# A decoder layer on one core: filter matrices kept in SBUF, v left unflipped, and half of the triangular inversion moved into the turns of the next phase

## What is computed

```python
q_in = silu(causal_dwconv(hidden_states @ Wq, wq_conv))        # the same for k_in and v_in
beta = jax.nn.sigmoid(hidden_states @ Wb)
# delta rule in chunks of 32 tokens, per batch and head:
inv = -(kb @ jnp.swapaxes(k, -1, -2)) * strict_lower
for i in range(1, chunk):
    inv = inv.at[..., i, :].add(jnp.einsum('...j,...jk->...k', inv[..., i, :], inv))
inv = inv + jnp.eye(chunk, dtype=q.dtype)
u = inv @ v
w = inv @ kb
...
local_long = causal_dwconv(v_in, fir_long.reshape(-1, fir_long.shape[-1])).reshape(B, L, H, dv)    # 64 taps
local_short = causal_dwconv(v_in, fir_short.reshape(-1, fir_short.shape[-1])).reshape(B, L, H, dv) # 5 taps
stats = jnp.concatenate([head_stats(t) for t in (local_short, local_long, delta_out, v_direct)], -1)
```

## Time and profile before

| | |
|---|---|
| time, median of 3 runs | 1316.88 us (1316.56 to 1321.13) |
| the profiled execution's own time | 1323.56 us |
| its span in the trace | 1321.8 us |
| granted PE clock, mean over the span | 0.895 of full speed |
| phase A, until the first instruction of B | 240.7 us |
| phase B | 240.7 to 319.5 us |
| phase CX, turns 0 and 1 | 319.5 to 362.4 us |
| busy share of the span | PE 85%, DVE 72%, ACT 68%, POOL 49% |

### The profile page before, as it was taken

The page is one execution under the profiler, slowest core; times in us unless marked ns, Lnnn a source line. Parts: engine busy times, 40 slices in busy tenths (PEclk is TensorE's granted clock), DMA queues, the critical chain, the costliest instruction groups (busy, mean ns, idle before and its releaser), DMA issues. The chain is left out here.

```text
span 1321.8 us, 28637 instructions
## 1 busy us (share of the span) xinstructions
PE 1119.9 (85%) x9251; PEld 820.2 (62%) x9251; DVE 958.0 (72%) x2132; ACT 898.0 (68%) x1743; POOL 653.0 (49%) x2200
## 2 busy tenths in 40 slices
PE   5998988783678799999999999999999888885756
PEld 4776766683566566766776776676677655443225
DVE  5999998698355657777877877777787566633985
ACT  5999998221344558787878878877887665453867
POOL 4777775563225544465465466547546543111007
PEclk9999998555557869999999999999999988897989
DMA  2443433893412434343433434343442342203106
GB/s 80 159 176 144 177 136 144 185 234 107 137 57 85 110 80 127 95 124 109 133 110 106 146 105 138 106 129 105 111 144 82 96 127 57 65 33 140 44 1 223
DMA packets 141779, 154.17 MB, mean 117 GB/s; under 512 B 48040, under 2 KB 106560, under 8 KB 141632
## 3 DMA queue, kind: packets, MB, share of 16 engines
q1 hardware_dynamic: 141632, 152.35, 38.4%
HBM read 93.32 MB, written 58.72 MB: 115 GB/s over the span
## 5 line engine op out<-in xcount | busy, mean ns | idle before, releaser
L2120 DVE TENSOR_REDUCE x_maxima<-x_psA 128x2 f32<-128x512 f32 x248 | 170.3, 687 | 96.2 <-PE x_psA L1448 93.7
L1704 ACT ACTIVATE x_PT<-x_psB 128x512 f32<-128x512 f32 x240 | 143.0, 596 | 56.5 <-PE x_psB L1472 52.1
L1711 ACT ACTIVATE x_psA<-x_mask_q 128x512 f32<-128x512 bf16 x239 | 142.4, 596 | 51.8 <-DVE x_maxima L2120 48.7
L297 DVE SCALAR_TENSOR_TENSOR a_conv<-a_ps_proj,taps,a_conv 128x253 f32<-128x253 f32 (+2 forms) x288 | 115.0, 471 | 8.4 <-ACT a_conv L364 8.4
L1448 PE MATMUL x_psA<-x_Ks,x_Qs 96*128 96x256 bf16 x496 | 99.5, 283 | 15.2 <-ACT x_psA L1711 14.7
L1469 PE MATMUL x_psB<-x_mask_k,x_ident_bf 128*128 128x512 bf16 x240 | 94.3, 393 | 13.0 <-ACT x_PT L1704 10.8
L533 PE MATMUL a_ps_proj<-a_hT,wqkv 128*128 128x256 f32 x384 | 93.2, 392 | 7.1 <-DVE a_conv L297 4.2
L1472 PE MATMUL x_psB<-x_Qs,x_Ks 98*128 98x256 bf16 x480 | 94.1, 277 | 0.0
L533 PEld LDWEIGHTS a_ps_proj<-a_hT,wqkv 128*128 128x128 f32 x384 | 71.5, 194 | 19.4 <-issue 6.6
L1864 POOL TENSOR_SCALAR x_parts_q<-x_rest 128x512 bf16<-128x512 f32 x16 | 23.9, 1494 | 116.3 <-DVE x_rest L2096 116.3
L1486 PE MATMUL x_psO<-x_PT,x_V 128*32 128x256 f32 x1024 | 72.0, 401 | 1.0 <-ACT x_PT L1704 1.0
(11 more groups left out here) (390 smaller groups left out, 3352.8 us busy)
## 6 DMA issues: line engine op xcount, KB each, us to landing
scratch_keypack<-a_keypack SPq DMA_DIRECT2D x16, 768.0 KB, 3.3
c_keypack<-scratch_keypack SPq DMA_DIRECT2D x16, 768.0 KB, 4.7
x_Ks<-scratch_k_parts SPq DMA_DIRECT2D x192, 64.0 KB, 2.2
b_matrix<-in_long_padded SPq DMA_DIRECT2D x16, 512.0 KB, 7.4
scratch_k_parts<-x_parts_k SPq DMA_DIRECT2D x32, 192.0 KB, 2.4
scratch_q_parts<-x_parts_q SPq DMA_DIRECT2D x32, 192.0 KB, 2.3
x_Qs<-scratch_q_parts SPq DMA_DIRECT2D x32, 192.0 KB, 3.0
a_x_in<-in_x SPq DMA_DIRECT2D x16, 256.0 KB, 2.7
```

Source lines behind the costliest of these rows:

```text
L297: nc.vector.scalar_tensor_tensor(acc, ps_proj[PROJ_BANK[p]][:, c, 0:L - j], taps[:, p, c, TAPS - 1 - j:TAPS - j], acc, ALU.mult, ALU.add). ...
L1704: nc.scalar.activation(PT[:, k % (2 * GROUP)], bank_B(b, k)[0], ACT.Exp, scale=XD ** -0.5).then_inc(pexp_ready, 1)
L1711: nc.scalar.activation(psA[:].rearrange("p t q -> p (t q)"), mask_q[:, k % 2].rearrange("p s k -> p (s k)"), ACT.Copy).then_inc(mask_writt ...
L2120: nc.vector.tensor_reduce(maxima[:, t, 2 * pair:2 * pair + 2], bank_A(b, k)[0], AX.X, ALU.max).then_inc(maxed, 1)
```

## The change

Four things are changed together.

1. In phase A v is no longer flipped: the two constants, `flipA`, `flipB`, `fA` and `fB` are gone. `vtok` copies straight into `v_windows`, and two SBUF-to-SBUF DMAs per turn (`win`) put the shifted half in place.
2. Phase A also brings the filter's matrices into SBUF, where they stay (`keep["matrix"]`, 256 channels x 64): in turns 1 to 4 one DMA each (`copy`) writes 16 copies of the padded taps to DRAM, and after that two DMAs per turn (`taps0`, `taps1`, 32 in all) read 256 KB each into 16 partitions in pieces of 256 bytes.
3. Phase B's filter has no loads any more. It is 256 matmuls (512 records) whose moving operand is 64 columns wide instead of 32 and whose stationary operand keeps its shape; the two channel halves alternate between the halves of the array's columns. ACT still copies 16 groups. `long` is stored in 8 DMAs of 512 KB in two stages, and B doesn't wait for them; SP waits before it loads `long` for batch 0 in CX, which now stands behind the 20 constant loads.
4. Phase B inverts groups 0 and 1 only, both on DVE as two interleaved single chains. The mask and the diagonal are 63 small memsets per group on POOL, which has no chain any more. Groups 2 and 3 are inverted in CX by DVE as a pair, in the pieces that `LATE_STEPS` lists, over turns 0 to 4.

```diff
-A_ORDER = [(0, "ld_x"), (4, "silu_v"), (1, "rstd"), (5, "kpk"), ...
+A_ORDER = [(0, "ld_x"), (1, "copy"), (4, "silu_v"), (1, "rstd"), (5, "kpk"), ...
...
+                elif op == "copy" and b < COPY_PARTS:
+                    first = b * D // COPY_PARTS
+                    sp.dma_start(dram["taps_copies"][first:first + D // COPY_PARTS],
+                                 bass.AP(dram["long_padded"].tensor, first * FIR_COLS,
+                                         [[FIR_COLS, D // COPY_PARTS], [0, COPIES], [1, FIR_COLS]])).then_inc(taps_copied[b * FC // COPY_PARTS], 16)
+                elif op in ("taps0", "taps1"):
+                    row, half = b % STEP, b // STEP
+                    first = half * P + int(op[-1]) * HB
+                    sp.wait_ge(taps_copied[half], 16 * COPY_PARTS // FC)
+                    taps_of = bass.AP(dram["taps_copies"].tensor, first * COPIES * FIR_COLS + P - 1 - row,
+                                      [[FIR_COLS - STEP, COPIES], [COPIES * FIR_COLS, HB], [1, HB]])
+                    sp.dma_start(keep["matrix"][row:P:STEP, first:first + HB], taps_of).then_inc(taps_placed, 16)
+                elif op == "win":
+                    sp.wait_ge(v_tok_ready, b + 1)
+                    sp.dma_start(keep["v_windows"][HB:P, 0, :, b], keep["v_windows"][0:HB, 1, :, b]).then_inc(window_set, 16)
+                    sp.dma_start(keep["v_windows"][0:HB, 0, 1, b], keep["v_windows"][HB:P, 1, 0, b]).then_inc(window_set, 16)
...
-                    nc.scalar.activation(v_tok[:], ps_tok[2][:], ACT.Copy).then_inc(v_tok_ready, 1)
-                elif op == "fA":
-                    act.wait_ge(v_flipped, b + 1)
-                    nc.scalar.activation(keep["v_windows"][:, 1, :, b], ps_tok[2][:], ACT.Copy).then_inc(flip_kept, 1)
...
+                    nc.scalar.activation(keep["v_windows"][:, 1, :, b], ps_tok[2][:], ACT.Copy).then_inc(v_tok_ready, 1)
...
-CG = 16
-GROUPS = D // CG
-DEPTH = 4
+EARLY_GROUPS = 2
+CHAIN_STEPS = 2 * (CH - 2)
+def substitution(M, product, j):
+    n, rows = M.shape[1], CH - 1 - j
+    return (product[:, :, 0:rows * j].rearrange("p q (i j) -> p q i j", j=j), M[:, :, j + 1:CH, 0:j],
+            M[:, :, j + 1:CH, j:j + 1].broadcast_to([P, n, rows, j]), M[:, :, j:j + 1, 0:j].broadcast_to([P, n, rows, j]))
+CG = 8
+GROUPS = P // CG
+DEPTH = 8
...
+            for stage in range(2):
+                sp.wait_ge(kept, (stage + 1) * (GROUPS // 2))
+                for half in range(FC):
+                    for part in range(2):
+                        at = slice(half * P + stage * HB, half * P + stage * HB + HB)
+                        sp.dma_start(dram["long_tok"][part * HB:part * HB + HB, :, :, at].rearrange("p t b c -> p (t b) c"),
+                                     keep["long"][half * HB:half * HB + HB, part, :, stage * HB:stage * HB + HB]).then_inc(long_stored, 16)
...
-                pe.wait_ge(loaded[n], 16 * (group // DEPTH + 1))
...
-                    for part in range(2):
-                        last = nc.tensor.matmul(psum[n][part * HB:part * HB + HB, c].rearrange("p t b -> p (t b)"),
-                                                matrix[n][:, c], keep["v_windows"][:, part, :, :, group * CG + c].rearrange("p t b -> p (t b)"),
+                for i in range(CG):
+                    for half in range(FC):
+                        c = half * P + group * CG + i
+                        last = nc.tensor.matmul(psum[n][half * HB:half * HB + HB, i], keep["matrix"][:, c],
+                                                keep["v_windows"][:, :, :, :, c].rearrange("p a t b -> p (a t b)"),
...
+            for q in range(EARLY_GROUPS):
+                pool.wait_ge(M_turned, q + 1)
+                for i in range(CH):
+                    nc.gpsimd.memset(M[q][:, i, i:i + 1], 1.0)
+                for i in range(CH - 1):
+                    last = nc.gpsimd.memset(M[q][:, i, i + 1:CH], 0.0)
+                last.then_inc(upper_cleared, 1)
...
+        LATE_STEPS = {(0, "b"): (1, 4), (1, "r"): (4, 9), (1, "d"): (9, 14), (1, "a"): (14, 15), (1, "s"): (15, 16), (2, "p"): (16, 17),
+                      (2, "d"): (17, 19), (2, "a"): (19, 21), (3, "k"): (21, 22), (3, "x"): (22, 23), (3, "q"): (23, 25),
+                      (3, "d"): (25, 26), (3, "a"): (26, 28), (3, "s"): (28, CH - 1)}
...
-            sp.dma_start(long[0][:], dram["long_tok"][:, :, 0]).then_inc(vs_loaded[0], 16)
...
+            sp.wait_ge(early["long_stored"], 128)
+            sp.dma_start(long[0][:], dram["long_tok"][:, :, 0]).then_inc(vs_loaded[0], 16)
...
+                    elif (b, op[3]) in LATE_STEPS:
+                        dve.wait_ge(inverse_step, LATE_GROUPS)
+                        for j in range(*LATE_STEPS[b, op[3]]):
+                            out, below, left, row = substitution(M, product, j)
+                            if j > 1:
+                                dve.wait_ge(inverse_step, LATE_GROUPS + 2 * j - 2)
+                            nc.vector.tensor_tensor(out, left, row, ALU.mult).then_inc(inverse_step, 1)
+                            dve.wait_ge(inverse_step, LATE_GROUPS + 2 * j - 1)
+                            nc.vector.tensor_tensor(below, below, out, ALU.add).then_inc(inverse_step, 1)
```

More of the change, by code:

```diff
@@ new lines, in _ @@
+            dve.wait_ge(M_turned, EARLY_GROUPS)
+            for j in range(1, CH - 1):
+                steps = [substitution(M[q][:].unsqueeze(1) if q == 0 else M[q].unsqueeze(1), products[q].unsqueeze(1), j) for q in range(EARLY_GROUPS)]
+                for q, (out, below, left, row) in enumerate(steps):
+                    if j > 1:
+                        dve.wait_ge(chain[q], 2 * j - 2)
+                    nc.vector.tensor_tensor(out, left, row, ALU.mult).then_inc(chain[q], 1)
+                for q, (out, below, left, row) in enumerate(steps):
+                    dve.wait_ge(chain[q], 2 * j - 1)
+                    nc.vector.tensor_tensor(below, below, out, ALU.add).then_inc(chain[q], 1)
@@ L805 @@
 MASKED = -1e30
-XW_LOADS = 16 * 7
+XW_LOADS = 16 * (7 + 13)
 STACKS = 2
```

258 lines of the change are left out of this document (107 added, 151 removed), and 18 rows, old and new, of the table C_ORDER.

## The result

The changed kernel takes 1309.06 us (median of 13 runs, 1303.55 to 1313.83), the kernel before 1317.64 (13 runs, 1315.10 to 1322.56). The ratio is 0.9929, 95% interval 0.9916 to 0.9942: 9 us faster, where 31 were forecast. The time lies outside the range of 1273 to 1306. The two profiled executions differ by more than the medians, 13.1 us in their spans, because that of the kernel before was 6.7 us longer than its median.

A forecast was written before the change was run, and what follows sets the result against it. The prediction took DVE's inversion to bound phase B, with PE's filter under it. Phase A -1.5, B -41 and CX +11.5 summed to -31 us: 1316.9 - 31 = 1286 us, range 1273 to 1306.

The forecast's parts named there:

- What bounds the kernel: Phase B: bound by DVE's inversion, busy 77.72 of 78.80 us, with PE's filter lying under it.
- inside the turns this is worth nothing: Phase A: removing PE records and ACT copies gains nothing within turns, only about 1.5 us after the last.
- cost 0: Phase A: the added SP issues and 512 KB of DMA per turn were priced at no time.
- The slow rival: Phase A, 3%: extra DMAs delay the load of x; landing 11.1 us after issue gives 1324 us.
- DVE's 37.8 us: Phase B: DVE's transposes, two interleaved chains, constants and a wait sum to 37.8 us against 78.7, a change of -41.
- by that row the moving columns cost nothing extra: Phase B filter: a CX row of the same shape gives 54 ns per record, so 512 records take 27.5 us.
- The filter rival: Phase B, 8%: moving columns set PE's pace, 107 ns per record, 55 us; B about 60 us, the whole 1308.
- The rival of late stores: Phase B into CX, 12%: at half the old rate the last stores land after 20 us, delaying `long`; 1294 us.
- +0.4 and +0.4: CX: waiting for batch 0's `long` costs 0.4 us on ACT at `c_U` and 0.4 at `rhs`.
- the moved work: CX: late transposes and steps, 39 us, lie mostly in DVE's gaps; CX grows by 11.5 us in all.
- 1.8 + 1.35: CX turns 0 and 1: two transposes delay `att0` by 1.8 us, step 14 delays the next by 1.35.
- 6.1 + 1.4: CX turns 2 to 4: delays of 2.6, 1 and 2.5 us, plus 1.4 for slower operations and shrinking gaps.

The follow-up runs named there:

- all_in_b: Changed kernel plus PE dummy matmuls in phase A, batch 0's `long` loaded before the constants, and all four groups inverted in phase B: 1318.82 us, ratio 1.0009.
- before_no_flips: Kernel before the change with only PE's flip matmuls left out of phase A; ACT still copies: 1325.06 us, ratio 1.0041.
- b_inner_const: Changed kernel plus PE dummy matmuls in phase A, batch 0's `long` before constants, batch innermost in `v_windows`, small constants and ACT's exponentials earlier: 1300.55 us, ratio 0.9852.
- b_contiguous: Changed kernel with filter matmuls reading 64 adjacent moving elements instead of 64 lying 1 KB apart: 1303.43 us, ratio 0.9873.
- long_first: Changed kernel with batch 0's `long` loaded ahead of the 20 constant loads in CX: 1303.97 us, ratio 0.9876.
- no_late_steps: Changed kernel plus PE dummy matmuls in phase A, batch 0's `long` before constants, and the late groups' 30 steps left out: 1296.06 us, ratio 0.9829.

## Why the prediction was wrong, by its own steps

- **What bounds the kernel: right.** B was DVE's, and all_in_b shows that without moving the two groups out nothing is gained.
- **Phase A, "inside the turns this is worth nothing" and "cost 0": the step that failed first.** The end did get shorter (from POOL's last `a_var_eps`, at 184.62 before and 189.84 after, B begins 56.1 and 55.4 us later), but by 0.7 us and not 1.5, and the turns took 5 us more. I treated work taken from PE as free. With it gone PE's clock went from 1.00 to 0.89 and the phase got longer: before_no_flips shows both without any other edit. +4.5 instead of -1.5, 6.0 us off in these two profiles (5.5 with the mean of 244.7). Whether it is the lower clock itself that lengthens the turns, and how, is not shown. The slow rival blamed the load of x. In the first turns DVE did stand 6.4 us for one, at 14.0 us, but by 38.9 us POOL's turns were level with those before (39.1); from there on no load of x was waited for.
- **Phase B, DVE's 37.8 us: right.** 37.4 in b_inner_const and 38.0 for the whole phase in b_contiguous.
- **Phase B, "by that row the moving columns cost nothing extra": failed.** The row has the shape and the weights, but its moving operand is adjacent in SBUF, and the filter's elements lie 1 KB apart. 73.4 ns per record instead of 53.7, although the clock was at 1.00 for nearly all of it and the row's at 0.50. For adjacent elements the row's price was right at 0.50 and nearly halves at 1.00 (b_contiguous). The filter rival priced the other end (107 ns) by the number of columns, which is not what makes the difference here, and the truth lay between. PE took 37.6 us instead of 27.5, and three things went with it that I had put under cover: DVE's wait for ACT was 3.0 instead of 0.5; two transposes took 2.4 instead of 1.9 each; and the stores' issue came out at the end. Of the 9.2 us of B beyond the sum, 2.5 + 1.0 + 0.4 lie before DVE's end and 5.2 behind it.
- **The stores: I priced their landing and left out their issue.** The last four issues kept SP for 7.95 us. The rival of late stores did not happen: SP issued `long` right behind the last constant and never waited for them. Its premise was in part right. The DMA line of the changed kernel, GB/s in slices of 2 us from 240 us on, shows 194 to 213 in the first stage:

```profile
GB/s 0 393 0 38 177 384 345 32 0 0 0 0 8 194 200 198 213 196 60 0 0 0 129 204 193 213 194 191 70 27 64 197 280 282 182 339 394 139 16 4
```

The prediction's old rate, 2048 KB in 10.2 us, is the middle of two stores: the first landed after 11.4 us beside loads of matrices, the second, alone, after 8.9. Window of the kernel before while only that second store ran:

```profile
307.00:313.00 6.00, 0.00 (x0) 0.00 (x0) 5.78 (x9) 0.00 (x0) 0.00 (x0) 0.50 1.02 290
```

In 512-byte pieces the stores ran at 290 GB/s, in 256-byte pieces at about 200: the rate fell by three tenths, not by half. The rule of 512 bytes that the prediction took from the page "DMA: Bandwidth & Descriptors" of the Trainium skill, section "Specifications", agrees with the traces in its direction; the halving was the prediction's own.

- **CX, `long` of batch 0, "+0.4 and +0.4": failed.** I followed ACT and not DVE, where sums of `long` stand ahead of the next `tt` and of steps 4 to 8; SP reached the load 14.2 us into CX instead of 12 (its first constants' issues stood behind the stores'), and it landed after 5.7 us instead of 3.5. Measured by long_first: 8.2 us instead of 0.8, 7.4 off.
- **CX, the moved work: right.** Without the wait for `long`, turns 0 and 1 take 45.5 us instead of 42.6, +2.9 where 1.8 + 1.35 stood. Turns 2 to 4 took 125.4 to 129.6 us in the three kernels without late groups (mean 128.0) and 132.6 to 136.6 in the eleven with their steps (mean 135.1): +7, where 6.1 + 1.4 stood. Much of that is not the steps: without them turns 2 to 4 still take 132.9 (no_late_steps, 134.1 with them). The steps alone cost 4.7 in the total (6.3 expected).
- **The sum.** -31 + 6.0 + 9.2 + 7.4 = -8.4, beside -8.6 between the medians. So close a match is luck: the terms are read from profiles whose spans differ by 13.1 us, and in the changed kernel's own profile turns 2 to 4 are only 3.0 us longer, where the forecast's 7.5 is left in the sum.

## What to carry to other kernels

A row prices a matmul only if its operands lie in memory as the new one's do: compare the step between moving elements, not only the shape. The same edit can decide whether a higher clock is worth anything. When work is taken off PE, look at the granted clock of that stretch, since what is left may run slower and shift every engine's timing. And a transfer has three times: when its queue's engine gets to it, how long the issue holds that engine (longer when others are under way), and how long it takes to land; a load that is moved behind others has to be followed to every engine that reads it.
